# Counting edges by node and type elsewhere than in the sorts' permutations, in a four-layer graph kernel on one NeuronCore

## The chip, the cores and the metric

The kernel runs on 1 core of one Trainium2 chip. The metric is the device time of one execution in microseconds; of several runs the median is taken.

## The reference, cut to what matters

A graph of 3125 nodes and 50000 edges (src, dst, and a type of nine) passes four layers: ARMA convolution, GCN, a relational layer with two directions, and neighbour sums. Each sums rows of other nodes over the edges. The change touches what is prepared for them once: how many edges of each type leave and enter each node.

```python
seg = jnp.concatenate([edge_type * n + edge_index[0], (edge_type + R) * n + edge_index[1]])
count = jax.ops.segment_sum(ones, seg, num_segments=2 * R * n).reshape(2 * R, n, 1)
cnt = jnp.maximum(count, 1.0)
...
deg = jax.ops.segment_sum(jnp.ones(src.shape[0], jnp.float32), dst, num_segments=n)
dinv = jnp.where(deg > 0, jax.lax.rsqrt(jnp.maximum(deg, 1.0)), 0.0)
```

The relational layer divides by cnt and adds count times a bias; the first two layers scale by dinv, which comes from the counts by destination, summed over the types.

## The kernel before, in words

Nodes lie in 25 tiles of 128. All work runs in stages, one after the other, each with its own instruction stream for each engine and semaphores between them; there is no planner, the order is that of the code.

First the 50000 edges are sorted twice. `rank_stage` finds each edge's place (chunk and slot) in the list sorted by tile; `Permute` moves the edges there. The first sort (key 1) goes by destination, over 400 columns of 125 edges; the second (key 0) by source, over the 416 columns of the list that the first one left. `Permute.run_stage` takes U = 16 columns a turn, in two buffers: VectorE makes one-hots of 16 columns in one operation each (line 450: place, chunk, local, group) and weights the first WEIGHED = 8 columns' place one-hots with the edge's high value (line 459), ScalarE weights the other eight and all low values (lines 475, 477), and TensorE makes three matmuls for a column (lines 492, 496, 498): high and low, by chunk, 416 columns wide, and local by group, 225 wide. The last one counts edges by node (128 local places) and by tile and type (25 x 9 groups): in the first sort by destination, in the second by source. VectorE may begin a turn when TensorE has ended the turn two before (`moved`).

`end_stage` decodes the sorted list and copies the counts. `degree_stage` stands between the sorts and makes dinv from the counts by destination. The second `rank_stage` also turns x (7 groups of four tiles) and spreads dinv along a row (7 groups, 50 passes of line 367) on TensorE, evicted by ScalarE, before its ranking matmuls.

`staircase_stage` (lines 944 to 1161) lays out 576 items, each a chunk of the list with a block of 512 source nodes in a tile of destination nodes or the reverse; TensorE picks each item's values from the turned list (line 1035). It also lists the nodes with many edges (`heavy`, `clone`, lines 1104 to 1161). `pair_counts_stage` then adds up, for each of the 576 items, a one-hot of the source with a one-hot of the target, a matmul of 512 columns (line 1225) into a place of PSUM that is known only at run time. TensorE's sequencer loads such places from a table, 16 registers for DOZEN = 12 items (`load`, line 1187), and waits each FOUR = 4 items for VectorE (`made`, line 1222) and ScalarE (`freed`, line 1223). VectorE makes a target one-hot an item (line 1203) and source one-hots for 16 items at once (line 1199). ScalarE evicts finished blocks (line 1249) and clears PSUM (line 1237); SP and POOL store them to two tables.

`dense_stage` is the matmul of a table of pair counts with rows (line 1609); its first use, `sum_x`, also gathers the rows of the heavy nodes from both tables (POOL, lines 1480 and 1481), cuts their counts in two (line 1707) and writes the rest back. Each loop turn n takes one block of 128 rows, brought by SP in a ring of four (line 1531); VectorE runs steps of `beside` (the factors of the typed layer) in between.

## Time and profile before

| | |
|---|---|
| time, median of 3 runs | 4890.89 us (4884.92 to 4891.96) |
| span of the profiled execution, first to last instruction | 4357.4 us |
| the median less that span (the page has no time of the profiled execution beside its span) | 533.5 us |
| first sort's turns, 51 to 270 us | VectorE 209.69 busy, TensorE 196.12 |
| second sort's turns, 324.7 to 553 us | VectorE 219.28 busy, TensorE 202.35 |
| pair counts, 588 to 793 us | VectorE 194.96 busy, TensorE 144.86 |
| mean granted clock of TensorE | 0.783 |

Busy times are those of operations; loads of registers, address computations, waits and branches of a sequencer count as none, though they take time. They stand in the trace under their line with a q behind the engine (PEldq is TensorE's sequencer). PEclk is the granted clock as a share of 2.4 GHz. Times in the views are microseconds from the span's start, durations in a list of instructions nanoseconds.

### The profile page before, as it was taken

Reading aid. Unit: us, or ns where it says so; the run is one execution under the profiler, and the core shown is the slowest. Engines: PE = TensorE matmul, PEld = TensorE weight load, DVE = VectorE, ACT = ScalarE, POOL = GpSimd, SP = SyncE. Lnnn points to the kernel's source line nnn. Section 1 sums busy time; section 2 is a strip of 40 time slices with the busy share of each in tenths; the row PEclk is TensorE's granted clock in tenths of the full one; section 3 lists DMA queues with packets and bytes.
Section 4 is the critical chain, followed back from the end, with each engine's and each line's share of the span. In section 5 each row is a group of like instructions: output and inputs, shape, how many; then the busy total and the mean of one; then the engine's idle time right before and its main releaser. Section 6 shows DMA issues by size and latency. Waiting matters only on the chain. (4 is left out here: it accounts for less than half of the span.)

```text
span 4357.4 us, 56067 instructions
## 1 busy us (share of the span) xinstructions
PE 3257.6 (75%) x16061; PEld 2561.3 (59%) x16062; DVE 2284.6 (52%) x3880; ACT 1437.0 (33%) x2751; POOL 1758.1 (40%) x1969
## 2 busy tenths in 40 slices
PE   6978966689999879998993787866674644444459
PEld 3545522559999677796862676755552533333348
DVE  8989999514445643355683555543454622222224
ACT  5848848546666564564500000000000000000005
POOL 0000012101111011120166777777756777777751
PEclk8989989899999989999995656555577855555569
DMA  4000025828888475694673111122245111212226
GB/s 156 0 0 0 0 106 206 266 80 288 289 288 291 142 276 177 233 313 142 232 284 98 49 53 53 53 53 52 53 177 183 52 52 52 53 52 53 53 68 205
DMA packets 161460, 569.88 MB, mean 131 GB/s; under 512 B 46176, under 2 KB 54721, under 8 KB 160908
## 3 DMA queue, kind: packets, MB, share of 16 engines
q1 hardware_dynamic: 89494, 394.83, 26.2%
q0 software_dynamic: 71408, 172.45, 13.2%
q8 instruction: 77, 1.26, 0.1%
q14 instruction: 91, 0.75, 0.1%
q10 hardware_dynamic: 390, 0.60, 0.0%
HBM read 405.06 MB, written 162.66 MB: 130 GB/s over the span
## 5 line engine op out<-in xcount | busy, mean ns | idle before, releaser
L2027 PE MATMUL ps_sum_rgcn<-gathered_rgcn,select_sum_rgcn 128*128 x3328 | 972.3, 440 | 560.1 <-SPq L1918 492.0
L2027 PEld LDWEIGHTS ps_sum_rgcn<-gathered_rgcn,select_sum_rgcn 128*128 128x128 f32 x3328 | 762.0, 308 | 625.6 <-issue 624.5
L1609 PE MATMUL ps_sum_arma<-pair_counts_f_sum_arma,parts_sum_arma 128*128 128x448 f32 (+1 forms) x3850 | 856.7, 374 | 13.6 <-ACT pair_counts_f_sum_arma L1650 13.6
L1943 POOL DMA_INDIRECT gathered_rgcn<-by_dst,row x782 | 739.4, 946 | 238.4 <-issue 218.3
L1609 PEld LDWEIGHTS ps_sum_arma<-pair_counts_f_sum_arma,parts_sum_arma 128*128 128x128 f32 x3850 | 707.1, 189 | 72.2 <-issue 14.2
L1943 POOL DMA_INDIRECT gathered_rgcn<-by_src,row x558 | 527.6, 945 | 198.1 <-issue 154.2
L2066 ACT COPY acc_rgcn<-ps_sum_rgcn 128x128 f32<-128x128 f32 x100 | 26.6, 266 | 1639.4 <-PE ps_sum_rgcn L2027 1639.4
L1488 POOL DMA_DIRECT2D rows<-parts_sum_arma x275 | 153.2, 558 | 896.3 <-DVE parts_sum_arma L1697 855.7
L2103 DVE TENSOR_TENSOR select_sum_rgcn<-one_hot_sum_rgcn,ps_coef_sum_rgcn 128x2048 f32<-128x2048 bf16 x52 | 118.9, 2287 | 576.0 <-PE ps_sum_rgcn L2027 575.9
L477 ACT ACTIVATE low_one_hot_sort<-place_one_hot_sort,low_in_sort 128x128 f16<-128x128 f16 (+1 forms) x816 | 300.0, 425 | 124.4 <-DVE place_one_hot_sort L450 124.4
L492 PE MATMUL ps_sort<-chunk_one_hot_sort,high_one_hot_sort 128*128 128x416 f16 (+1 forms) x816 | 283.9, 348 | 46.7 <-DVE group_one_hot_sort L450 46.7
L1952 PE MATMUL ps_turn_sum_rgcn<-ident,one_hot_sum_rgcn 128*128 128x128 bf16 x832 | 245.2, 302 | 94.1 <-DVE one_hot_sum_rgcn L2075 41.8
L496 PE MATMUL ps_sort<-chunk_one_hot_sort,low_one_hot_sort 128*128 128x416 f16 (+1 forms) x816 | 282.5, 346 | 0.0
L2080 DVE COPY turned_sum_rgcn<-ps_turn_sum_rgcn 128x1024 bf16<-128x1024 bf16 x104 | 71.5, 688 | 386.3 <-PE ps_got_sum_rgcn L1959 353.8
L693 POOL DMA_INDIRECT gathered_rgcn<-by_src,row x224 | 216.5, 966 | 136.1 <-ACTq L759 71.2
L1650 ACT CAST pair_counts_f_sum_arma<-blocks_arma_mid 128x1792 fp32r<-128x1792 f16 x125 | 211.3, 1690 | 133.9 <-PE ps_sum_arma L1609 126.3
L2075 DVE TENSOR_TENSOR one_hot_sum_rgcn<-local,ps_iota_sum_rgcn 128x2048 bf16<-128x2048 f32 x104 | 237.4, 2284 | 7.4 <-DVE select_sum_rgcn L2103 1.8
L1000 POOL IOTA after_iota_staircase<- 128x128 f16 x1 | 0.2, 243 | 551.9 <-POOLq L509 551.9
L498 PE MATMUL ps_sort<-group_one_hot_sort,local_one_hot_sort 128*128 128x225 f16 (+1 forms) x816 | 215.3, 264 | 0.0
L1650 ACT CAST pair_counts_f_sum_arma<-axT_arma 128x1792 fp32r<-128x1792 f16 x100 | 169.1, 1691 | 124.6 <-PE ps_sum_arma L1609 119.5
L1959 PE MATMUL ps_got_sum_rgcn<-factor_parts,turned_sum_rgcn 128*128 x832 | 183.3, 223 | 20.8 <-DVE turned_sum_rgcn L2080 17.2
L1712 DVE CAST pair_counts_f_sum_arma<-blocks_arma_mid 128x1334 fp32r<-128x1334 f16 x125 | 106.9, 855 | 170.8 <-PE ps_sum_arma L1609 164.8
(458 smaller groups left out, 5283.9 us busy)
## 6 DMA issues: line engine op xcount, KB each, us to landing
blocks_arma_mid<-pairs SPq DMA_DIRECT2D x125, 800.0 KB, 5.9
axT_arma<-pairs SPq DMA_DIRECT2D x100, 800.0 KB, 5.9
pair_counts_arma_sum<-pairs SPq DMA_DIRECT2D x50, 800.0 KB, 6.0
rows<-parts_sum_arma POOLq DMA_DIRECT2D x275, 128.0 KB, 5.3
by_src<-rows_rgcn_tables SPq DMA_DIRECT2D x50, 576.0 KB, 3.8
by_dst<-rows_rgcn_tables SPq DMA_DIRECT2D x50, 576.0 KB, 3.8
exact<-whole_pairs SPq DMA_DIRECT2D x25, 800.0 KB, 3.3
pairs<-whole_pairs POOLq DMA_DIRECT2D x25, 800.0 KB, 5.5
```

Source lines behind the costliest of these rows:

```text
L477: nc.scalar.activation(self.low[e, parity, u // 2, :, u % 2], place, ACT.Copy, scale=o.low_in[e, bass.ds(i * U + u, 1)]).then_inc(self.wei ...
L492: nc.tensor.matmul(self.ps[:, 0, 0:C], self.high[e, parity, pair, :, at], chunk, start=False, stop=False)
L496: nc.tensor.matmul(self.ps[:, 1, 0:C], self.low[e, parity, pair, :, at], chunk, start=False, stop=False)
L498: nc.tensor.matmul(self.ps[:, 2, 0:self.G], self.local[e, parity, pair, :, at], self.group[e, parity, pair, :, at], start=False, stop=Fals ...
L693: nc.gpsimd.indirect_dma_start(got[:, n, :], None, tables[0].rearrange("n (r f) -> (n r) f", f=D), bass.IndirectOffsetOnAxis(ap=k.orders[0 ...
L1609: last = nc.tensor.matmul(ps[:, g, 0:here.stop - here.start], half(part), counts[:, n % 2, here].bitcast(F32R), start=t == 0 and part == 0 ...
L1650: nc.scalar.copy(counts[:, n % 2, 0:CUT].bitcast(F32R), ring[n % RING][:, 0:CUT]).then_inc(raised, 1)
L1943: nc.gpsimd.indirect_dma_start(got[:, n % PLACES, :], None, table, bass.IndirectOffsetOnAxis(ap=o.row[:, n % C:n % C + 1], axis=0)).then_i ...
L1952: inst = nc.tensor.transpose(ps_turn[:, half, v, :], hot[:, parity, half * OCTET + v, :], k.ident16[:, :])
L1959: inst = nc.tensor.matmul(ps_got[:, parity, at:at + PARTS * R], turned[:, half, v, :], parts[:, bass.ds(tile, 1), :, :].rearrange("p a q r ...
L2027: nc.tensor.matmul(ps[:, bass.ds(slot, P)], select[:, parity, u, :], rows[:, bass.ds(place, D)], start=False, stop=False, skip_group_check ...
L2075: nc.vector.tensor_tensor(hot[:, parity, :, :], k.local[:, bass.ds(first, U), None].to_broadcast([P, U, P]), ps_iota[:, None, 0:P].to_broa ...
```

## The change

The counts leave `Permute` in the form that they had, and come from two other places.

- **By destination (`k.count[:, :, R:]`), in the second sort.** Its columns come from the list sorted by destination, so that a column has one tile. The 225-wide group one-hot becomes one of 9 types (`type_in`), and the matmul of 9 columns goes to the tile's place in PSUM, `count_at`, of which 16 are loaded each turn. The first sort makes no counts at all: it has two matmuls a column. The weighting on VectorE grows to 14 columns of 16 in the first and 10 in the second sort.
- **By source (`k.count[:, :, 0:R]`), in the pair counts.** For each of the 576 items a second matmul, 9 columns wide, of the same source one-hot with a one-hot of the type (`typed`, made for 16 items at once), goes to a place from a second table `q.count_at`, 16 registers loaded for 12 items. The types of the items are a third pick in `staircase_stage`; edges outside the item's block get type 0 there, which no one-hot names.
- `degree_stage` goes; dinv is made at the end of the second sort. Its row is made in `staircase_stage`, no longer in `rank_stage`.
- The list of heavy nodes needs the counts by source and moves into `sum_x`, spread over its loop turns 4 to 11. The two gathers go from the start of POOL's queue to before its thirteenth store, the write back from SP's turn 9 to turn 21.

```diff
@@ rank_stage
-            nc.vector.tensor_copy(o.local_in[e, :], ints[e, 1, :])
-            nc.vector.scalar_tensor_tensor(o.group_in[e, :], tile_of[e, :], float(R), k.edges[e, 2, :], ALU.mult, ALU.add)
...
-            nc.vector.scalar_tensor_tensor(o.group_in[e, :], tile_of[e, :], float(R), l.type[e, :], ALU.mult, ALU.add)
+            nc.vector.tensor_copy(o.local_in[e, :], l.local[e, :])
+            nc.vector.tensor_copy(o.type_in[e, :], l.type[e, :])
+            nc.vector.tensor_scalar(o.count_at[:, :], l.tile_of_chunk[:, :], float(R), float(2 * SPAN), ALU.mult, ALU.add)
...
-                for g in range(2 * FOURS):
+                for g in range(FOURS):
                     tiles = four(g)
                     act.wait_ge(grouped, g + 1)
-                    to = k.xT if g < FOURS else k.dinv_row
-                    nc.scalar.copy(to[:, tiles.start * P:tiles.stop * P], ps[:, 3 + g % B, 0:len(tiles) * P]).then_inc(evicted, 1)
 @block.tensor
...
-                        place = ps[:, 3 + g % B, v * P:v * P + P]
-                        if g < FOURS:
-                            last = nc.tensor.transpose(place, k.xcur[:, t, :], k.ident[:, :])
-                        else:
-                            last = nc.tensor.matmul(place, k.ident[0:NT, t:t + 1].to_broadcast([NT, P]), dinvT[:, :],
-                                                    start=True, stop=True)
+                        last = nc.tensor.transpose(ps[:, 3 + g % B, v * P:v * P + P], k.xcur[:, t, :], k.ident[:, :])
                     last.then_inc(grouped, 1)
@@ Permute
+        self.weighed = 14 if o.key else 10
...
-                    compare(self.chunk, o.chunk_in, C)
-                    compare(self.local, o.local_in, P)
+                    if not o.key:
+                        compare(self.local, o.local_in, P)
+                        compare(self.type, o.type_in, R)
                     dve.wait_ge(self.placed, i + 1)
-                    nc.vector.tensor_tensor(self.high[e, parity, 0:self.WEIGHED // 2, :, :],
-                                            self.place[e, parity, 0:self.WEIGHED // 2, :, :],
-                                            columns(o.high_in, P, self.WEIGHED), ALU.mult)
-                    compare(self.group, o.group_in, self.G).then_inc(self.made, 1)
+                    nc.vector.tensor_tensor(self.high[e, parity, 0:self.weighed // 2, :, :],
+                                            self.place[e, parity, 0:self.weighed // 2, :, :],
+                                            columns(o.high_in, P, self.weighed), ALU.mult)
+                    compare(self.chunk, o.chunk_in, C).then_inc(self.made, 1)
...
+                    if not o.key:
+                        count_at = nc.values_load_multi_w_load_instructions(
+                            o.count_at[0:1, bass.ds(i * U, U)], engines=(PE,), min_val=2 * SPAN,
+                            max_val=2 * SPAN + (NT - 1) * R,
+                            skip_runtime_bounds_check_because="made from tiles below NT")[1]
                     pe.wait_ge(self.made, i + 1)
                     for u in range(U):
                         pair, at = divmod(u, 2)
                         chunk = self.chunk[e, parity, pair, :, at]
-                        if u >= self.WEIGHED:
+                        if u >= self.weighed:
                             pe.wait_ge(self.weighted, i * U + u + 1)
                         nc.tensor.matmul(self.ps[:, 0, 0:C], self.high[e, parity, pair, :, at], chunk, start=False,
                                          stop=False)
-                        if u < self.WEIGHED:
+                        if not o.key:
+                            nc.tensor.matmul(banks[:, bass.ds(count_at[u], R)], self.local[e, parity, pair, :, at],
+                                             self.type[e, parity, pair, :, at], start=False, stop=False,
+                                             skip_group_check=True)
+                        if u < self.weighed:
                             pe.wait_ge(self.weighted, i * U + u + 1)
                         nc.tensor.matmul(self.ps[:, 1, 0:C], self.low[e, parity, pair, :, at], chunk, start=False,
-                                         stop=False)
-                        nc.tensor.matmul(self.ps[:, 2, 0:self.G], self.local[e, parity, pair, :, at],
-                                         self.group[e, parity, pair, :, at], start=False, stop=False).then_inc(self.moved, 1)
-
+                                         stop=False).then_inc(self.moved, 1)
+
+                banks = self.ps[:, :, :].rearrange("p b w -> p (b w)")
                 nc.tensor.sem_inc(self.moved, 2 * U)
@@ end_stage
+                    then(nc.vector.tensor_copy(k.count[:, :, R:S2], ps[:, 2, 0:NT * R].rearrange("p (t r) -> p t r", r=R)))
+                    then(nc.vector.tensor_reduce(deg[:, :], k.count[:, :, R:S2], AX.X, ALU.add))
+                    nc.vector.tensor_scalar(has[:, :], deg[:, :], 0.0, None, ALU.is_gt)
+                    nc.vector.tensor_scalar_max(roots[:, 0, :], deg[:, :], 1.0)
+                    nc.vector.tensor_scalar(roots[:, 1, :], deg[:, :], 1.0, None, ALU.add).then_inc(rooting, 1)
...
-def degree_stage(nc, k):
...
@@ staircase_stage
+            pe.wait_ge(kept, 1)
             pe.wait_ge(moved, 1)
+            for g in range(FOURS):
+                if g >= 2:
+                    pe.wait_ge(evicted, g - 1)
+                for v, t in enumerate(four(g)):
+                    last = nc.tensor.matmul(ps[:, 6 + g % 2, v * P:v * P + P], k.ident[0:NT, t:t + 1].to_broadcast([NT, P]),
+                                            dinvT[:, :], start=True, stop=True)
+                last.then_inc(grouped, 1)
...
-            for n in (0, 1):
+            pe.wait_ge(evicted, FOURS)
+            for n in (0, 1, 2):
+                if n == 2:
+                    pe.wait_ge(shown, 1)
                 for first, w, bank in ((0, SPAN, 1), (SPAN, ITEMS - SPAN, 2)):
                     for h in range(QUARTERS):
-                        last = nc.tensor.matmul(ps[:, 5 * n + bank, 0:w], turned[:, n, h, :], pick[:, h, first:first + w],
+                        last = nc.tensor.matmul(ps[:, 5 * (n % 2) + bank, 0:w], turned[:, n, h, :], pick[:, h, first:first + w],
                                                 start=(h == 0), stop=(h == QUARTERS - 1))
-            last.then_inc(laid, 1)
-            pe.wait_ge(reached, 1)
-            nc.tensor.matmul(ps[0:1, 4, P:P + U], row[:, :], k.ident[0:U, 0:U], start=True, stop=True).then_inc(lined, 1)
-            pe.wait_ge(cloned, 1)
-            for t in range(NT):
-                last = nc.tensor.matmul(ps[:, 5, 2 * LOW:2 * LOW + 2], clone[:, t, :], place[:, t, :], start=(t == 0),
-                                        stop=(t == NT - 1))
-            last.then_inc(placed, 1)
...
+            last_target.then_inc(shown, 1)
+            dve.wait_ge(shown, 1)
+            then(nc.vector.tensor_scalar(inside[:, :], q.target_at[:, :], 0.0, None, ALU.is_ge))
+            then(nc.vector.scalar_tensor_tensor(inside[:, :], q.target_at[:, :], float(SPAN), inside[:, :], ALU.is_lt, ALU.mult))
+            dve.wait_ge(laid, 2)
+            for first, w, bank in ((0, SPAN, 1), (SPAN, ITEMS - SPAN, 2)):
+                here = slice(first, first + w)
+                nc.vector.tensor_tensor(q.type_at[:, here], inside[:, here], ps[:, bank, 0:w], ALU.mult)
@@ pair_counts_stage
+                    nc.vector.tensor_tensor(
+                        typed[:, n // V % 2, :, :, :],
+                        q.type_at[:, n:n + V].rearrange("p (a b) -> p a b", b=2)[:, :, None, :].to_broadcast([P, V // 2, R, 2]),
+                        q.steps[:, None, 1:R + 1, :].to_broadcast([P, V // 2, R, 2]), ALU.is_equal)
...
+                        counts = load(PE, count_at, i * (BODY // DOZEN * ROW) + u // DOZEN * ROW, ROW,
+                                      SPANS * SPAN + (NT - 1) * R)
                     if u % FOUR == 0:
 
                         pe.wait_ge(made, i * BODY + u + FOUR)
                         pe.wait_ge(freed, frees[u % DOZEN // FOUR])
                         nc.tensor.nop(nofuse=True)
+                    nc.tensor.matmul(ps[:, bass.ds(counts[u % DOZEN], R)], source[:, u // V % 2, u % V // 2, :, u % 2],
+                                     typed[:, u // V % 2, u % V // 2, :, u % 2], start=False, stop=False, skip_group_check=True)
                     nc.tensor.matmul(ps[:, bass.ds(table[u % DOZEN], SPAN)], source[:, u // V % 2, u % V // 2, :, u % 2],
                                      target[:, u % V, :], start=False, stop=False, skip_group_check=True).then_inc(multiplied, 1)
@@ dense_stage
-    CLONED = 9
+    HEAVY, LISTED, CLONED, CUTOUT, REPLACED = 4, 7, 12, 17, 21
...
-            if exact is not None:
-                at = bass.IndirectOffsetOnAxis(ap=k.clone_node[:, 0:1], axis=0)
-                nc.gpsimd.indirect_dma_start(clone_whole[:, :], None, exact[:, :], at).then_inc(k.cloned, 16)
-                nc.gpsimd.indirect_dma_start(clone_half[:, :], None, pairs[:, :], at).then_inc(k.cloned, 16)
             for b in range(M):
                 if b:
                     gp.wait_ge(fetched, 16 * (fetched_before + b))
                 for t in range(NT):
                     m = b * NT + t
+                    if exact is not None and m == CLONED:
+                        gp.wait_ge(listed, 1)
+                        at = bass.IndirectOffsetOnAxis(ap=k.clone_node[:, 0:1], axis=0)
+                        nc.gpsimd.indirect_dma_start(clone_whole[:, :], None, exact[:, :], at).then_inc(k.cloned, 16)
+                        nc.gpsimd.indirect_dma_start(clone_half[:, :], None, pairs[:, :], at).then_inc(k.cloned, 16)
                     gp.wait_ge(split, m + 1)
...
+                if exact is not None and n == HEAVY + 1:
+                    pe.wait_ge(ready, 1)
+                    nc.tensor.matmul(ps[:, 7, 0:NT], ones[:, :], heavy16[:, :], start=True, stop=True)
+                    nc.tensor.matmul(ps[:, 7, LOW:LOW + NT], before[:, :], heavy16[:, :], start=True, stop=True).then_inc(counted, 1)
+                if exact is not None and n == LISTED + 2:
+                    pe.wait_ge(cloned, 1)
+                    for i in range(NT):
+                        last = nc.tensor.matmul(ps[:, 7, 2 * LOW:2 * LOW + 2], clone[:, i, :], place[:, i, :], start=(i == 0),
+                                                stop=(i == NT - 1))
+                    last.then_inc(placed, 1)
...
+            def list_heavy():
+
+                dve.wait_ge(counted, 1)
+                then(nc.vector.tensor_copy(heavy_of[:, :], ps[:, 7, 0:NT]))
+                then(nc.vector.tensor_tensor_scan(upto[:, :], heavy_of[:, :], heavy_of[:, :], 0.0, ALU.add, ALU.max))
+                then(nc.vector.tensor_tensor(upto[:, :], upto[:, :], heavy_of[:, :], ALU.subtract))
+                then(nc.vector.tensor_tensor(upto[:, :], upto[:, :], ps[:, 7, LOW:LOW + NT], ALU.add))
+                then(nc.vector.scalar_tensor_tensor(where[:, :], upto[:, :], float(LAST + 1), heavy[:, :], ALU.add, ALU.mult))
+
+            def place_heavy():
+
+                then(nc.vector.tensor_tensor(clone[:, :, :], after_iota[:, None, :].to_broadcast([P, NT, P]),
+                                             where[:, :, None].to_broadcast([P, NT, P]), ALU.is_equal))
+                nc.vector.tensor_tensor(clone[0:LAST, NT - 1, :], clone[0:LAST, NT - 1, :], k.ident16[0:LAST, :],
+                                        ALU.add).then_inc(cloned, 1)
+
+            def name_heavy():
+
+                dve.wait_ge(placed, 1)
+                then(nc.vector.tensor_copy(found[:, :], ps[:, 7, 2 * LOW:2 * LOW + 2]))
+                nc.vector.scalar_tensor_tensor(k.clone_node[:, :], found[:, 1:2], float(P), found[:, 0:1], ALU.mult,
+                                               ALU.add).then_inc(listed, 1)
...
-                if n >= RING:
+                if exact is not None and n == HEAVY:
+                    find_heavy()
+                elif exact is not None and n == LISTED:
+                    list_heavy()
+                elif exact is not None and n == LISTED + 1:
+                    place_heavy()
+                elif exact is not None and n == LISTED + 4:
+                    name_heavy()
+                elif n >= RING:
                     next(apart, None)
                     next(apart, None)
```

## Rows read from the trace of the kernel before

**Rows 1.** Busy time by engine in stretches of the first 800 us, clock and DMA share behind
```profile
core 0: us, PE busy (x) PEld busy (x) DVE busy (x) ACT busy (x) POOL busy (x), PEclk, DMA share, GB/s
51.00:270.00 219.00, 196.12 (x1206) 116.17 (x1204) 209.69 (x129) 179.14 (x600) 0.00 (x0) 0.97 0.01 4
277.61:280.46 2.85, 0.00 (x1) 0.03 (x1) 1.44 (x9) 1.53 (x2) 0.00 (x0) 0.61 0.00 0
324.70:553.00 228.30, 202.35 (x1254) 121.48 (x1252) 219.28 (x137) 186.35 (x624) 0.00 (x0) 0.97 0.00 0
553.00:588.00 35.00, 13.34 (x77) 7.27 (x77) 32.15 (x89) 2.16 (x4) 2.98 (x4) 0.57 0.00 1
588.00:793.00 205.00, 144.86 (x583) 59.31 (x583) 194.96 (x614) 162.74 (x347) 46.55 (x24) 0.94 0.49 192
```

**Rows 2.** Timeline of VectorE, one turn of the first sort: start us, duration us
```profile
77.40 1.22 DVE L450 TENSOR_TENSOR place_one_hot_sort<-slot_in_sort,steps_sorts 125x2048 f16<-125x2048 f16 x1
78.53 3.62 DVE L450 TENSOR_TENSOR chunk_one_hot_sort<-chunk_in_sort,steps_sorts 125x6656 f16<-125x6656 f16 x1
82.07 1.22 DVE L450 TENSOR_TENSOR local_one_hot_sort<-local_in_sort,steps_sorts 125x2048 f16<-125x2048 f16 x1
83.20 0.68 DVE L459 TENSOR_TENSOR high_one_hot_sort<-place_one_hot_sort,high_in_sort 125x1024 f16<-125x1024 f16 x1
83.81 2.02 DVE L450 TENSOR_TENSOR group_one_hot_sort<-group_in_sort,steps_sorts 125x3600 f16<-125x3600 f16 x1
85.75 1.22 DVE L450 TENSOR_TENSOR place_one_hot_sort<-slot_in_sort,steps_sorts 125x2048 f16<-125x2048 f16 x1
```

**Rows 3.** Timeline of TensorE, one item of a turn
```profile
535.17 0.34 PE L492 MATMUL ps_sort<-chunk_one_hot_sort,high_one_hot_sort 128*128 128x416 f16 x1
...
535.53 0.26 PE L498 MATMUL ps_sort<-group_one_hot_sort,local_one_hot_sort 128*128 128x225 f16 x1
535.63 0.34 PE L492 MATMUL ps_sort<-chunk_one_hot_sort,high_one_hot_sort 128*128 128x416 f16 x1
```

**Rows 4.** Timeline of ScalarE, two activations of a turn
```profile
72.80 0.42 ACT L475 ACTIVATE high_one_hot_sort<-place_one_hot_sort,high_scale_sort 125x128 f16<-125x128 f16 x1
73.09 0.42 ACT L477 ACTIVATE low_one_hot_sort<-place_one_hot_sort,low_in_sort 125x128 f16<-125x128 f16 x1
```

**Rows 5.** Instructions of lines 1225, 1187, 588:793: ns min/median/max, first and last start
```profile
L1225 PEldq FUSED_REGOPS  x576: 37/37/37, 591.3 to 791.0; - x192
...
L1225 PE MATMUL ps_pairs<-target_one_hot_pairs,source_one_hot_pairs x576: 379/379/634, 592.1 to 792.9; 128*128 128x512 f16 x192
...
L1187 PEldq TENSOR_LOAD <-item_at_adjacency x48: 1102/1232/3373, 589.3 to 786.4; - x48
```

**Rows 6.** Instructions of line 1225, one dozen (640.7:642.75)
```profile
L1225 PEldq FUSED_REGOPS  x12: 37/37/37, 640.8 to 642.7; - x12
```

**Rows 7.** Timeline of TensorE in the pair counts, two dozens
```profile
633.63 2.76 PE L1225 MATMUL ps_pairs<-target_one_hot_pairs,source_one_hot_pairs 128*128 128x512 f16 x12 [0.83 <-DVE target_one_hot_pairs L1203]
637.22 2.76 PE L1225 MATMUL ps_pairs<-target_one_hot_pairs,source_one_hot_pairs 128*128 128x512 f16 x12 [0.83 <-DVE target_one_hot_pairs L1203]
```

**Rows 8.** Timeline of the staircase, VectorE's and TensorE's largest operations of the clone list
```profile
581.17 3.49 DVE L1140 TENSOR_TENSOR clone_staircase<-after_iota_staircase,clone_row_staircase 128x3200 bf16<-128x3200 f16 x1
...
584.97 0.79 PE L1042 MATMUL ps_staircase<-node_place_staircase,clone_staircase 128*128 128x2 bf16 x25 [2.71 <-DVE clone_staircase L1142]
```

**Rows 9.** Timeline of the second ranking, TensorE and VectorE
```profile
294.93 7.59 PE L367 MATMUL ps_rank<-dinv_turned_rank,ident 25*128 25x128 f32 x50
...
303.91 1.28 DVE L316 COPY best_rank<-ps_rank 128x416 f32<-128x416 f32 x2 [5.63 <-PE ps_rank L395]
```

**Rows 10.** Instructions of lines 1992 and 1967, neighbouring loads in the typed sum
```profile
L1992 PEldq TENSOR_LOAD <-ring_late x1: 1113/1113/1113, 2364.0 to 2364.0; - x1
...
L1967 PEldq TENSOR_LOAD <-look_at_late x1: 1110/1110/1110, 2365.3 to 2365.3; - x1
```

**Rows 11.** The first sum: timeline of ScalarE, and busy times of a later stretch
```profile
831.41 1.69 ACT L1650 CAST pair_counts_f_sum_x<-pair_counts_sum_x 128x1792 fp32r<-128x1792 f16 x1 [12.93 <-DMA pair_counts_sum_x<-pairs]
...
850.00:860.00 10.00, 10.00 (x51) 9.28 (x50) 7.21 (x26) 7.97 (x8) 2.89 (x4) 1.00 1.02 418
```

212 lines of the change are left out of this document (103 added, 109 removed).

## The prediction

> **What bounds the kernel now.** I read the table of stretches first [rows 1], because the change touches only the first 900 us. In both sorts VectorE is busy for 96% of the stretch and TensorE for 89 to 90%; in the pair counts VectorE is busy for 95% and TensorE for 71%. By this view VectorE binds everywhere, and work taken from it should pay one for one. Then I asked for single turns. One turn of a sort takes 8.35 us from one place_one_hot to the next (77.40 to 85.75), with no gap between VectorE's five operations [rows 2]. TensorE spends 0.46 us on an item in it: 0.18 for each of the two 416-column matmuls, 0.10 for the 225-column one [rows 3], 16 items in 7.4 us. ScalarE issues one activation each 0.29 us [rows 4], 24 of them in 7.0 us.
>
> The pair counts need a second view, that of the sequencer's own instructions, since busy shares leave them out. For twelve items TensorE's sequencer makes one load of 16 registers, at least 1.10 us long, three groups of waits, and one address computation (FUSED_REGOPS) for each matmul [rows 5, 6]. Two neighbouring dozens start 3.59 us apart (633.63 to 637.22), of which the matmuls themselves take 2.76 with the last one's drain: this gap is not TensorE's array and not VectorE, which is named as releaser but works ahead [rows 7]. Twelve addresses stand in 1.9 us [rows 6], and three groups of waits account for two breaks of about 0.3 in it: 0.115 to 0.12 for an address with its matmul's dispatch. With 1.27 for a load and the address ahead of it, 1.27 + 3 x 0.30 + 12 x 0.115 = 3.55, so the sequencer alone explains 3.59. Forty-eight dozens give 172 us of the 203.6 from the first load to the last matmul (589.3 to 792.9) [rows 5]; VectorE is busy for 195 [rows 1]. Both nearly bind. The remaining 31 are long loads (median 1.23, longest 3.37 [rows 5]), the fill, loop ends and waits.
>
> **The first sort.** VectorE loses local_one_hot (1.14 from start to start) and group_one_hot (1.95), and its weighting grows from 8 to 14 columns: 0.60 becomes 1.00, by the slope between the 1024- and 2048-element operations (0.68 and 1.22). It now must wait for place_one_hot's end before weighting, 0.12 more. From turn start to TensorE's start: 1.26 + 1.00 + 3.62 + 0.05 = 5.93. TensorE loses the third matmul, 0.37 an item; from its first matmul to VectorE's release two turns on: 15 x 0.37 + 0.34 + 0.14 = 6.03. Two buffers make these a loop, (5.93 + 6.03) / 2 = 5.98 a turn, just above TensorE's own 5.92. ScalarE has 18 activations, 5.3 us, below it. 24 x (8.35 - 5.98) + 2.5 at the first fill + 1.6 in the last turn: -61 us.
>
> **The second sort.** VectorE keeps local, gains a 144-element compare (0.15, an estimate from the slope; bounds 0.1 and 0.3), weights 10 columns (0.73) and loses group: 1.14 + 1.14 + 0.15 + 0.73 + 3.53 = 6.69, 6.82 to TensorE's start. The 9-column matmul is nearest to the 2-column ones of the clone list, 25 in 0.79 us with the drain, so 0.025 to 0.03 each [rows 8]; upper bound the 0.10 of today's. An item is 0.40, and 15 x 0.40 + 0.21 + 0.48 = 6.67. (6.82 + 6.67) / 2 = 6.75. ScalarE's 22 activations are 6.5 us, close below. Here too TensorE's sequencer gets a load and 16 addresses a turn, 1.3 + 1.9 us, but its other 48 dispatches are static and it waits for VectorE anyway: hidden, priced at nothing. Were the cover gone, it would add at most 1.3 a turn, 34 us. 25 x (8.35 - 6.75) + 1.6 + 0.9: -42.5.
>
> The rule of the Trainium skill that bears on the small matmuls is in "TensorE: Matmul & The Clock Gate", Back-to-back issue gap: up to 64 columns a matmul costs an issue floor of about 25 ns. The row of 25 matmuls agrees (0.025), but its addresses are constants. By that rule the 576 new matmuls of the pair counts would cost 14 us in all, and the result would be the first rival below.
>
> **Between the sorts.** The degree stage goes: -2.55 (277.61 to 280.16, most of the stretch in [rows 1]). Its seven small VectorE operations enter the end of the second sort, +1.0; the square root's table load lies behind ScalarE's copies there. In the rank stage 50 matmul passes of the dinv rows held TensorE for 7.59 us and VectorE idle for 5.63 [rows 9]; without them the ranking starts when its parts are ready: -5.3, -0.6 because three short 416-column operations on VectorE replace three longer ones, -0.3 from a shorter queue of transposes. -6.2 together.
>
> **The staircase.** The clone list leaves (VectorE's 3.49 us compare and what stands around it, 579.90 to 584.84 [rows 8]): -4.9. In its place TensorE makes the dinv rows before the picks: at the rate of [rows 9] 50 passes take 5.6 us at 2.4 GHz and twice that at 1.2, and this stretch runs at 0.57 [rows 1]. So the picks start some 3 to 8 us later, and a third pick, its waits, and five operations on VectorE follow (about 3 us). Net +2, bounds 0 and +6.
>
> **The pair counts.** VectorE: one 144-element compare each 16 items, 36 x 0.15 = 5 us; if VectorE still bound, that were all. TensorE's array: 576 x 0.03, not binding at either clock level. The sequencer: a second load of 16 registers each dozen and a second address each item. Two neighbouring loads of 16 in the typed sum start at 2364.0 and 2365.3 [rows 10]: they do not overlap, 1.3 each, 1.27 with the sum above. An address is 0.115. A dozen grows by 1.27 + 12 x 0.115 = 2.65, from 3.59 to 6.24, above VectorE's 4.1 (195 / 48); 48 x 2.65 = 127. The old remainder of 31 stays, but for the 2 to 4 us in which the sequencer waited for VectorE or ScalarE. I take +125; bounds +5 (all hidden) and +150 (each load as long as the median 1.23 or more, and transfers lengthening twice as many loads). Queued behind it are ScalarE's evictions and the stores of the rows; they have slack, as their pace is set by the same matmuls.
>
> **The first sum.** The two gathers of clone rows leave its start, where ScalarE waits 12.9 us for the fifth block of pair counts behind the transfer of dinv_loop in pieces of one number each [rows 11]. That transfer stays; without 1.6 MB ahead of it (two gathers of 128 rows of 6400 bytes), it starts and ends about 4 us earlier, at the 418 GB/s of a later stretch. Moved to the thirteenth row store on POOL, the gathers wait for the list; row stores queue behind them, with eight buffers in hand. VectorE's 6.7 us of list work fall in a stretch in which TensorE is busy for 10.00 us of 10.00 and VectorE for 7.21 [rows 11]; the 25 small matmuls add 0.7. Net -3, bounds -6 and +4.
>
> **Sum.** -61 - 42.5 - 2.6 - 6.2 + 1.0 + 2 + 125 - 3 = +12.7. The profiled span is 4357.4; what lies around it, 533.5 by the median 4890.9, I leave unchanged: 4903.6.
>
> **Rivals.** (1) Other side, faster: the sequencer works ahead of the array, as it does in the sorts, and the new loads and addresses hide there; the pair counts grow by VectorE's 5 us only. Result 4890.9 - 112 + 5, about 4784 (by the page's floor 4793). Against it: 3.59 us is the sequencer's own sum. It decides below 112 us of growth, 2.34 us a dozen. Chance 0.08. (2) One of the two prices is not paid (the second load overlaps the first, 61 us, or an address shares its computation with its neighbour's, 66): about 4840. Chance 0.10. (3) The sorts gain less: three engines within 0.3 us of each other wait for one another in turn, 6.4 and 7.1 us a turn; +19, 4923. For it: the loop through both buffers already costs more than each engine. Chance 0.12. (4) Transfers lengthen the doubled loads by as much again as today (some 23 us): 4927. Chance 0.10. The forecast has 0.60, with its own range of 4890 to 4918.
>
> **Chances and range.** A measurement here tells a change of over 0.2% (9.8 us) from none. Of the forecast's 0.60, 0.35 lie above 4900.7, 0.23 within the bound, 0.02 below. Rivals 1 and 2 are faster, 3 and 4 slower but for 0.02. Faster 0.20, same 0.25, slower 0.55. Leaving out rivals 1 and 2, the range reaches from 4878 to 4928.
>
> **What would show it.** In the profile after: 5.9 to 6.1 us from one place_one_hot to the next in the first sort, 6.6 to 6.9 in the second; 6.2 to 6.4 us between dozens of pair matmuls, two TENSOR_LOADs a dozen, 1152 address computations with 0.115 between them, and VectorE idle there for a third of the time; some 325 us from first load to last matmul. The prediction is wrong if dozens stand under 5.9 us apart (faster), or if the pair stage keeps VectorE's pace.

## The result and the profile after

The changed kernel takes 4922.97 us (median of four, 4913.22 to 4924.57), the kernel before, measured along with it, 4891.43 (four runs, 4884.92 to 4896.42). The ratio is 1.0066 with a 95% interval of 1.005 to 1.0081: slower by 31.5 us (24 to 40 by the interval). The forecast was +12.7 us, with a range from 4878 to 4928.

First the busy times by engine of the changed kernel, in the stretches that answer to [rows 1]: the first sort's turns, what lies between the sorts, the second sort's turns with its end, the staircase, and the pair counts from the first register load to the last matmul. The columns are those of [rows 1]: busy time of TensorE, of its weight loads, of VectorE, ScalarE and POOL, then clock, DMA share and GB/s.

```profile
50.67:213.00 162.33, 152.06 (x804) 77.85 (x802) 147.30 (x82) 135.32 (x450) 0.00 (x0) 0.97 0.01 6
213.00:257.00 44.00, 29.80 (x129) 14.76 (x130) 38.73 (x111) 4.56 (x9) 0.00 (x0) 0.77 0.00 1
257.00:444.00 187.00, 172.61 (x1264) 94.48 (x1263) 178.27 (x143) 172.03 (x574) 0.00 (x0) 0.97 0.00 0
444.00:485.80 41.80, 24.54 (x106) 17.63 (x105) 30.23 (x84) 7.07 (x14) 2.83 (x3) 0.56 0.00 1
485.80:828.30 342.50, 217.43 (x1160) 106.92 (x1158) 215.69 (x648) 167.85 (x347) 15.37 (x24) 0.80 0.30 115
```

Two places changed much, in opposite directions. The second sort begins at 257.0 us where it began at 324.7, and the pair counts' first load stands at 485.8 where it stood at 589.3 [rows 5]: 103.5 us are won by then. The pair counts then take 342.1 us to their last matmul (485.8 to 827.9), not 203.6: 138.5 us are lost. No engine is busy in them for more than 217 us of 342. In [rows 1] VectorE was busy for 95% of this stretch; now it is for 63%, and TensorE, with twice the matmuls, for 63% too. What fills the rest stands in no column of this view.

It stands in the rows of the sequencer. These are the loads and address computations of the whole stage (count; shortest, median and longest in ns; first and last start in us), to be read beside [rows 5].

```profile
L1164 PEldq TENSOR_LOAD <-item_at_adjacency x48: 1102/1107/3538, 485.8 to 820.2; - x48
L1164 PEldq ALU_OP  x48: 36/36/36, 486.9 to 821.9; - x48
L1164 PEldq TENSOR_LOAD <-count_at_adjacency x48: 1100/1105/3292, 487.0 to 821.9; - x48
...
L1210 PEldq FUSED_REGOPS  x576: 37/37/37, 488.5 to 826.6; - x192
...
L1212 PEldq FUSED_REGOPS  x576: 37/37/37, 488.6 to 826.7; - x192
```

There are 96 loads and 1152 addresses, twice what there was. The same view for one dozen, between 577 and 586 us:

```profile
L1164 PEldq TENSOR_LOAD <-item_at_adjacency x2: 1107/2080/3052, 577.9 to 584.2; - x2
...
L1164 PEldq TENSOR_LOAD <-count_at_adjacency x1: 1105/1105/1105, 579.2 to 579.2; - x1
```

A dozen whose two loads are both short takes 6.3 us (577.9 to 584.2), and its second load begins 1.3 us after the first, when that has ended. Over all 48 dozens the closest two stand 6.21 us apart (3.57 before). The forecast for this spacing was 6.24. The median, which has long loads and waits in it, grew from 4.12 to 6.62. Some loads are long, though, up to 3.5 us: the 96 sum to 144.2 us, which is 38.2 above 96 x 1.105; the 48 of before summed to 76.6, 23.6 above 48 x 1.105.

The sorts, in VectorE's timeline (start us, duration us; idle time before it and what ended it in brackets). The first sort, two turns and the start of a third, beside [rows 2]:

```profile
149.84 1.22 DVE L435 TENSOR_TENSOR place_one_hot_sort<-slot_in_sort,steps_sorts 125x2048 f16<-125x2048 f16 x1 [0.37 <-PE ps_sort L491]
151.19 1.09 DVE L445 TENSOR_TENSOR high_one_hot_sort<-place_one_hot_sort,high_in_sort 125x1792 f16<-125x1792 f16 x1
152.20 3.62 DVE L435 TENSOR_TENSOR chunk_one_hot_sort<-chunk_in_sort,steps_sorts 125x6656 f16<-125x6656 f16 x1
155.73 1.23 DVE L435 TENSOR_TENSOR place_one_hot_sort<-slot_in_sort,steps_sorts 125x2048 f16<-125x2048 f16 x1
157.08 1.09 DVE L445 TENSOR_TENSOR high_one_hot_sort<-place_one_hot_sort,high_in_sort 125x1792 f16<-125x1792 f16 x1
158.09 3.62 DVE L435 TENSOR_TENSOR chunk_one_hot_sort<-chunk_in_sort,steps_sorts 125x6656 f16<-125x6656 f16 x1
162.07 1.23 DVE L435 TENSOR_TENSOR place_one_hot_sort<-slot_in_sort,steps_sorts 125x2048 f16<-125x2048 f16 x1 [0.36 <-PE ps_sort L491]
```

Lengths of 5.89 (149.84 to 155.73) and 6.34 us (155.73 to 162.07) alternate, 6.11 on average. One is VectorE's own length; in every other it waits 0.36 us for TensorE to release the buffer. The second sort, one turn:

```profile
352.86 1.23 DVE L435 TENSOR_TENSOR place_one_hot_sort<-slot_in_sort,steps_sorts 128x2048 f16<-128x2048 f16 x1
354.00 1.22 DVE L435 TENSOR_TENSOR local_one_hot_sort<-local_in_sort,steps_sorts 128x2048 f16<-128x2048 f16 x1
355.14 0.22 DVE L435 TENSOR_TENSOR type_one_hot_sort<-type_in_sort,steps_sorts 128x144 f16<-128x144 f16 x1
355.28 0.82 DVE L445 TENSOR_TENSOR high_one_hot_sort<-place_one_hot_sort,high_in_sort 128x1280 f16<-128x1280 f16 x1
356.02 3.62 DVE L435 TENSOR_TENSOR chunk_one_hot_sort<-chunk_in_sort,steps_sorts 128x6656 f16<-128x6656 f16 x1
359.55 1.22 DVE L435 TENSOR_TENSOR place_one_hot_sort<-slot_in_sort,steps_sorts 128x2048 f16<-128x2048 f16 x1
```

It takes 6.69 us; with its neighbour of 6.74 the mean is 6.72. The compare of types takes 0.14 from start to start.

Last, TensorE in the staircase, beside [rows 8, 9].

```profile
463.12 11.03 PE L1002 MATMUL ps_staircase<-dinv_turned_staircase,ident 25*128 25x128 f32 x50
...
474.66 4.00 PE L1014 MATMUL ps_staircase<-pick_staircase,turned_staircase 104*128 104x512 f16 x16 [0.20 <-ACT wide_row L1033]
...
480.17 2.10 PE L1014 MATMUL ps_staircase<-pick_staircase,turned_staircase 104*128 104x512 f16 x8 [1.38 <-DVE target_at_adjacency L1117]
```

The 50 matmul passes of dinv's rows, 7.59 us in the second ranking, take 11.03 here, where the mean granted clock is 0.56 of 2.4 GHz, near the lower level of 1.2. The passes start 0.213 us apart here; in the second ranking of before some 30 of the 50 stood 0.112 apart, the others 0.213. The picks wait behind them, and the third pick comes only after a wait of 1.38 us for VectorE.

### The profile page after: what moved, and what is told of

Same layout as the page of the kernel before. It is cut to its first block and busy times, and to the rows that moved or that the text cites. A ratio compares the mean times of both kernels' runs of the same rounds, so it can differ in the third digit from the quotient of the medians.

```text
span 4911.9 us, 57120 instructions
## 1 busy us (share of the span) xinstructions
PE 3303.8 (67%) x16248; PEld 2538.4 (52%) x16249; DVE 2205.5 (45%) x3872; ACT 1384.1 (28%) x2550; POOL 1725.5 (35%) x1968
## 5 line engine op out<-in xcount | busy, mean ns | idle before, releaser
L2082 PE MATMUL ps_sum_rgcn<-gathered_rgcn,select_sum_rgcn 128*128 x3328 | 962.3, 422 | 649.3 <-issue 596.6
L2082 PEld LDWEIGHTS ps_sum_rgcn<-gathered_rgcn,select_sum_rgcn 128*128 128x128 f32 x3328 | 739.5, 291 | 729.6 <-issue 726.3
L2014 PEld LDWEIGHTS ps_got_sum_rgcn<-factor_parts,turned_sum_rgcn 128*128 128x128 bf16 x832 | 113.7, 137 | 372.1 <-issue 332.3
L463 ACT ACTIVATE low_one_hot_sort<-place_one_hot_sort,low_in_sort 128x128 f16<-128x128 f16 (+1 forms) x816 | 273.3, 425 | 87.7 <-DVE place_one_hot_sort L435 86.1
L716 DVE TENSOR_TENSOR rows_rgcn_tables<-ps_rgcn_tables,typed_bias_late 128x384 f32<-128x384 f32 x300 | 162.8, 556 | 182.8 <-remote 94.4
L1184 DVE TENSOR_SCALAR target_one_hot_pairs<-wide_adjacency,target_at_adjacency 128x512 f16<-128x512 f16 x576 | 170.0, 347 | 83.3 <-PE ps_pairs L1212 70.5
```

The costliest lines, as they stand in the source:

```text
L463: nc.scalar.activation(self.low[e, parity, u // 2, :, u % 2], place, ACT.Copy, scale=o.low_in[e, bass.ds(i * U + u, 1)]).then_inc(self.wei ...
L1184: nc.vector.tensor_scalar(target[:, n % V, :], q.wide[:, :], q.target_at[:, n:n + 1], None, ALU.is_equal).then_inc(made, 1)
L2014: inst = nc.tensor.matmul(ps_got[:, parity, at:at + PARTS * R], turned[:, half, v, :], parts[:, bass.ds(tile, 1), :, :].rearrange("p a q r ...
L2082: nc.tensor.matmul(ps[:, bass.ds(slot, P)], select[:, parity, u, :], rows[:, bass.ds(place, D)], start=False, stop=False, skip_group_check ...
```

## The experiments

All of them are made from the changed kernel, but for the first, which is the kernel before once more.

**A second trace of the kernel before.** The first trace's span, 4357.4 us, did not fit the runs' 4891.

> The kernel before, unchanged, for a second trace. The profiled span of before was 4357.4 us against a median of 4891, and that of the changed kernel 4911.9 against 4923. If the first trace was the odd one, this one shows a typed sum about 2337 us long (first to last instruction), as the changed kernel has, and not 1868; up to the typed sum its stages should stand within 1 us of the first trace. If the changed kernel's typed sum is slower because of the change, it shows 1868 again.

It took 4901.44 us with a span of 4900.1. The typed sum in the first trace of before, in this one, and in the changed kernel, in the view of stretches:

```profile
2352.00:4222.00 1870.00, 1128.99 (x5371) 943.97 (x5371) 736.44 (x690) 57.12 (x207) 1375.21 (x1452) 0.58 0.24 68
```

```profile
2406.00:4765.00 2359.00, 1153.16 (x5371) 933.29 (x5371) 739.24 (x690) 56.79 (x207) 1373.31 (x1452) 0.59 0.19 54
```

```profile
2434.00:4773.00 2339.00, 1139.58 (x5373) 922.15 (x5374) 739.42 (x690) 56.62 (x207) 1373.62 (x1452) 0.60 0.20 55
```

The last two last some 2335 to 2355 us, with nearly the same busy times as the first, which had 1866. Up to the pair counts' last matmul the two traces of before differ by 0.3 us (792.9 and 792.6), at the end of the first sum by 2.9. So the first trace is sound for the stages that the argument rests on. The second half of the expectation did not hold all the way: the stage ahead of the typed sum, which makes its tables, took 215 us (2194.1 to 2409.3) and not 165 (2190.8 to 2355.4). The 533.5 us that the prediction laid around the span lay inside it in a usual execution: some 490 us are time that the typed sum lacked in that first one, some 50 time that its tables lacked. Why, these runs do not show. The later stages also differ by some 20 us between two usual traces, so that only the first 930 us are compared trace with trace here, and the total by the medians.

**No counts by source.** The second load, the count matmul and the one-hot of types are left out; the counts by source stay zero.

```diff
-                        counts = load(PE, count_at, ...)
...
-                    nc.tensor.matmul(ps[:, bass.ds(counts[u % DOZEN], R)], source[...], typed[...], ...)
```

> The changed kernel without the counts by source (no second load, no count matmul, no one-hot of types; these counts stay zero). Theory of the sequencer's sum: dozens 3.6 us apart, 204 us from the first load to the last matmul, as before the change, and a total of about 4923 - 138 = 4785 us. Rival, that something else in the changed kernel (the third pick, the clock after a shorter second sort) slows the pair counts: over 215 us.

4780.09 us, ratio to before 0.9779 (0.9758 to 0.98). The stage takes 202.0 us from first load to last matmul (487.4 to 689.4), its closest dozens stand 3.57 us apart. So the loss lies wholly in what the change adds here, and all the rest of the change is worth 110 us. The rival, something else in the changed kernel, is refuted.

**A constant place, no load.**

```diff
-                        counts = load(PE, count_at, ...)
...
-                    nc.tensor.matmul(ps[:, bass.ds(counts[u % DOZEN], R)], source[...], typed[...], ...)
+                    nc.tensor.matmul(ps[:, SPANS * SPAN:SPANS * SPAN + R], source[...], typed[...], ...)
```

> The changed kernel with the count matmul at one constant place and without its load (all counts by source fall into the first tile's place). Theory: loads and address computations are the cost, not the matmuls; a constant matmul costs the sequencer 0 to 0.06 us, so dozens stand 3.6 to 4.3 us apart and the stage takes 204 to 220 us, near VectorE's own 200. Rival, any second matmul costs the 0.115 us: 5.0 us a dozen, about 267 us.

```profile
485.60:697.60 212.00, 165.21 (x1160) 77.68 (x1158) 198.89 (x648) 162.82 (x347) 44.66 (x24) 0.93 0.48 186
```

212.0 us with all 1160 matmuls, each with its own load of weights (1158 in the second column). Five hundred and seventy-six matmuls of 9 columns, their weight loads and 36 compares cost 10 us against none. Neither the array nor the weights are what costs 138. VectorE is busy for 94%, almost without a pause, as before the change.

**A place from a register, no load.** The two runs differ in whether the count matmul's place can share the address of the pair matmul.

```diff
-                    nc.tensor.matmul(ps[:, bass.ds(counts[u % DOZEN], R)], source[...], typed[...], ...)
+                    nc.tensor.matmul(ps[:, bass.ds(table[u % DOZEN], R)], source[...], typed[...], ...)
```

> The changed kernel without the second load; the count matmul takes its place from the item's own register (it adds into the pair counts, which are then wrong, and counts by source stay zero). Theory: 24 addresses a dozen, 3.59 + 12 x 0.115 = 4.97 us apart, stage about 48 x 4.97 + 28 = 267 us. Rival, an address is shared with its neighbour or hidden: 3.6 to 4.2 us and 204 to 215 us.

The stage took 207.8 us (486.2 to 694.0), as the rival has it. But the rows show that the run did not do what it was made for: the only address computations stand under the count matmul's line, and the pair matmul has none.

```profile
L1208 PEldq FUSED_REGOPS  x576: 37/37/37, 488.4 to 692.0; - x192
```

Two matmuls from one register use one computation. Hence the second form:

```diff
+        beside = ps[:, 16:(SPANS + 1) * SPAN]
...
+                    nc.tensor.matmul(beside[:, bass.ds(table[u % DOZEN], R)], source[...], typed[...], ...)
```

> The changed kernel without the second load; the count matmul takes the item's own register, but 16 columns further on, so that its place has to be computed by itself (the pair counts are wrong by it, counts by source stay zero). In the run with the shared register the trace had one address computation an item. Theory of the sequencer's sum: with two an item, 12 x 0.115 more, 4.97 us a dozen, about 48 x 4.97 + 28 = 267 us. Rival, the second computation hides: 208 to 215 us, as with the shared one.

```profile
L1210 PEldq FUSED_REGOPS  x576: 46/46/51, 487.5 to 766.6; - x192
...
L1212 PEldq FUSED_REGOPS  x576: 37/42/42, 487.6 to 766.7; - x192
```

281.6 us (485.3 to 766.9), 73.8 more than with the shared address, and again with 48 loads only. Its closest dozens stand 5.12 us apart, not 4.97. The address computations of an item last 46 and 42 ns here where the changed kernel's last 37 and 37, and follow each other after 0.120 and 0.124 us, not 0.115. That is 0.17 us a dozen, close to the 0.15 more; why they are longer was not tested. The second address of an item is paid in full.

**The second load.** The first attempt kept the load and gave the matmul a constant place.

```diff
-                    nc.tensor.matmul(ps[:, bass.ds(counts[u % DOZEN], R)], source[...], typed[...], ...)
+                    nc.tensor.matmul(ps[:, SPANS * SPAN:SPANS * SPAN + R], source[...], typed[...], ...)
```

> The changed kernel with its second load, but the count matmul at one constant place (all counts by source fall into the first tile's place). The two runs before showed 212 us for the stage with neither, 208 with the item's address shared. Theory: a second load adds 1.20 us to a dozen of 3.6 to 3.7, so 4.9 us at least, and about 48 x 4.9 + some 40 us of long loads = 275 us; VectorE, at 4.1 a dozen, no longer binds. Rival, a load by itself hides behind the array's work and only the pair of load and address is dear: under 225 us.

215.3 us, and only this load in its trace, 48 times:

```profile
L1164 PEldq TENSOR_LOAD <-item_at_adjacency x48: 1102/1196/3332, 486.3 to 695.0; - x48
```

The load whose registers nobody reads is not in the trace. The run therefore says nothing of the load; it is the run without load once more, and shows how far two traces of that may differ (212.0 and 215.3). So one address of each dozen was taken from the table:

```diff
+                    at = bass.ds(counts[0], R) if u % DOZEN == 0 else slice(SPANS * SPAN, SPANS * SPAN + R)
+                    nc.tensor.matmul(ps[:, at], source[...], typed[...], ...)
```

> The second load for real: in the run with the constant place its registers were used nowhere and the trace shows 48 loads, not 96. Here the first count matmul of each dozen takes its place from the loaded table and the other eleven a constant one (most counts by source fall into the first tile's place). Theory of the sequencer's sum: 1.27 for the load and 0.115 for one address on top of 3.6 to 3.7 us, 5.0 a dozen; stage 48 x 5.0 + some 35 us of long loads = 275 us. That is 63 above the 212 with neither; the changed kernel's 342 less the 281.6 with an address of its own gives 60.5 for the same load. Rival, the load hides when its registers are hardly used: under 230.

```profile
L1164 PEldq TENSOR_LOAD <-count_at_adjacency x48: 1100/1105/3516, 486.6 to 767.3; - x48
```

288.3 us, 13 more than expected and 76.3 more than the 212.0 without load and address. The closest dozens stand 5.00 us apart, as expected. What was too low is the time of long loads: the 96 loads sum to 147.6 us, 41.6 above 96 x 1.105, where the run without the second load had 26.0 above its 48 x 1.105.

**Stores out of the way.** The 50 transfers of finished rows (two of 0.8 MB for each of 25 tiles) wait until the last row is taken, and ScalarE no longer waits for a stored buffer before it fills it again. They then send the buffers of the last two rows; the tables in memory lack the others.

```diff
-                        act.wait_ge(kept[i % 2], (i // 2) * 16)
-                        act.wait_ge(stored[i % 2], (i // 2) * 16)
+                        pass
...
-                gp.wait_ge(taken, (i + 1) * SPANS)
+                gp.wait_ge(taken, NT * SPANS)
...
-                sp.wait_ge(taken, (i + 1) * SPANS)
+                sp.wait_ge(taken, NT * SPANS)
```

> The changed kernel with all 50 row stores of the pair counts issued after the last row is taken (they then store the last two rows' buffers, so the pair counts in memory are wrong). Theory: the store transfers are what lengthens register loads; without them all 96 loads take 1.10 to 1.11 us, the 38 us above that go, and the stage from first load to last matmul takes about 304 us; the stores follow after it, so the total is longer or equal. Rival, loads are long for another reason (the loop's turn, instruction fetch): 342 again.

```profile
L1164 PEldq TENSOR_LOAD <-item_at_adjacency x48: 1102/1105/1108, 487.8 to 784.5; - x48
...
L1164 PEldq TENSOR_LOAD <-count_at_adjacency x48: 1100/1105/1105, 489.1 to 785.8; - x48
```

and, in the view of stretches, from the first load to the last matmul:

```profile
487.80:791.60 303.80, 207.88 (x1159) 108.43 (x1158) 213.27 (x648) 167.82 (x347) 0.00 (x0) 0.85 0.00 0
```

Not one load is longer than 1.11 us, and the stage takes 303.8 us, 38.3 less than with the stores. This is the clearest row of the study: 48 x 6.25 = 300 us by the sequencer's sum (6.25 is the median here, 6.22 the closest), at VectorE 70% and TensorE 68% busy. The whole kernel takes 4951.59 us, since the stores now stand in front of the first sum.

**Narrower loads.**

```diff
-                        counts = load(PE, count_at, i * (BODY // DOZEN * ROW) + u // DOZEN * ROW, ROW, ...)
+                        counts = load(PE, count_at, i * (BODY // DOZEN * ROW) + u // DOZEN * ROW, DOZEN, ...)
```

> The changed kernel, its second load taking the 12 registers that are used and not 16. By the slope between loads of 16 registers (1.10 us) and of 8 to 9 (0.55) in the trace of before, 0.069 us a register: 0.28 us less a dozen, 5.98 apart, stage about 13 us shorter, 329. Rival, a load has one price whatever its width: 342 again.

```profile
L1164 PEldq TENSOR_LOAD <-count_at_adjacency x48: 845/848/2659, 488.2 to 810.1; - x48
```

329.0 us (486.9 to 815.9), 13.1 less, where two traces of the same pair counts differ by 2 (342.1 and, in the run on the second sort below, 344.1). Four registers fewer save 0.257 us, 0.064 each. The total of this one run, 4911.48 us, is 11.5 below the changed kernel's median, within the spread of single runs.

**The second sort's load and addresses.** The prediction priced them at nothing.

```diff
-                        count_at = nc.values_load_multi_w_load_instructions(o.count_at[0:1, bass.ds(i * U, U)], ...)
...
-                            nc.tensor.matmul(banks[:, bass.ds(count_at[u], R)], self.local[...], self.type[...], ...)
+                            nc.tensor.matmul(banks[:, 2 * SPAN:2 * SPAN + R], self.local[...], self.type[...], ...)
```

> The changed kernel with the count matmul of the second sort at one constant place, without its load of 16 registers (counts by destination wrong). The prediction priced load and addresses there at nothing, as VectorE and the array bind at 6.7 us a turn. Theory: the turn stays at 6.71 us within 0.05. Rival, part of the sequencer's 3.1 us a turn shows: 6.4 or less, 8 us or more over 26 turns.

```profile
352.76 1.23 DVE L435 TENSOR_TENSOR place_one_hot_sort<-slot_in_sort,steps_sorts 128x2048 f16<-128x2048 f16 x1
...
359.46 1.23 DVE L435 TENSOR_TENSOR place_one_hot_sort<-slot_in_sort,steps_sorts 128x2048 f16<-128x2048 f16 x1
```

Turns of 6.70 and 6.74 us, mean 6.72, with and without; from the first turn's start to the last's it is 169.8 us here and 169.7 in the changed kernel. There the trace has 26 loads and 416 addresses, and they cost nothing that these runs can tell:

```profile
L473 PEldq TENSOR_LOAD <-count_at_sort x26: 1102/1106/1294, 257.1 to 430.9; - x26
...
L486 PEldq FUSED_REGOPS  x416: 37/37/37, 263.8 to 437.3; - x139
```

**Keep the half that pays.** Counts by destination come from the second sort, as in the changed kernel; counts by source from the first, 225 columns wide, as the kernel before made those by destination there. The pair counts and the staircase make none, and the third pick is gone.

```diff
+            nc.vector.tensor_copy(o.local_in[e, :], ints[e, 2, :])
+            nc.vector.scalar_tensor_tensor(o.group_in[e, :], ints[e, 3, :], float(R), k.edges[e, 2, :], ALU.mult, ALU.add)
...
+                        if o.key:
+                            low = nc.tensor.matmul(self.ps[:, 2, 0:NT * R], self.local[...], self.type[...], ...)
```

> A version that keeps the half that pays: counts by destination in the second sort as in the changed kernel; counts by source in the first sort, 225 columns wide, as the kernel before counts there by destination; none in the pair counts, and no third pick. Against the changed kernel: first sort's turns back to 8.35 us (+54), pair counts back to 203 us (-138), third pick gone (-3): 4923 - 87 = 4836 us, 0.989 of before. Rival, that the sorts' gain is one of both sorts together or that the longer first sort costs more than in the kernel before (its source codes are made in the first ranking): 4860 or more.

Its stretches: first sort's turns and end, second sort's, pair counts.

```profile
50.60:265.00 214.40, 191.85 (x1180) 113.94 (x1179) 208.93 (x125) 179.13 (x600) 0.00 (x0) 0.97 0.01 4
314.60:502.00 187.40, 173.32 (x1261) 95.20 (x1260) 178.27 (x142) 171.60 (x573) 0.00 (x0) 0.96 0.00 0
540.90:749.30 208.40, 149.71 (x583) 60.63 (x582) 194.59 (x612) 162.77 (x347) 40.24 (x24) 0.92 0.48 189
```

4841.01 us where 4836 was expected, 0.9902 of the kernel before (0.9883 to 0.9922), 82 us below the changed kernel. Turns are 8.35 us in the first sort and 6.72 in the second, the pair counts take 208.4.

## Why the prediction came out as it did

The direction, the mechanism and the outer range (4878 to 4928) held; the size did not. The measured +31.5 us is two and a half times the forecast +12.7, and 4922.97 lies above the forecast's own range of 4890 to 4918, where the prediction had put rivals 3 (4923) and 4 (4927). That it falls on rival 3's figure is chance, as the terms show. In the traces the loss at the last matmul of the pair counts is 35.0 us (827.9 against 792.9). Term by term:

- **Sorts, degree stage and ranking**: forecast -61 - 2.6 - 6.2 = -69.8 up to the second sort's start, measured -67.7 (257.0 against 324.7). The turn is 6.11 us and not 5.98. The loop through both buffers that the prediction computed is there, as the alternating 5.89 and 6.34 show, but it is longer than reckoned: 6.03 us from a turn's start to TensorE's first matmul (forecast 5.93) and 6.20 from there to the release (forecast 6.03), together 0.27 for two turns; 24 turns make 3 us of it.
- **Second sort, its end and the staircase**: forecast -42.5 + 1.0 + 2 = -39.5, measured -35.8 (228.8 us from the sort's start to the first load, 264.6 before). The turn is right, 6.72 against 6.75 (15 x 0.40 + 0.21 + 0.48 is 6.69 and not 6.67, which moves the 6.75 by 0.01 at most), and so is the load priced at nothing, as its own run shows. The staircase is what was too cheap: the dinv rows stand ahead of the picks for 11.03 us, the upper of the two rates that the prediction named, and VectorE waits 3.9 us at their end where the old kernel had work on the clone list. From the second sort's last matmul to the first load it is 46.1 us, 39.0 before: 7.1 more where +3 was forecast (+1.0 at the sort's end, +2 here). With the +1.0 as forecast the staircase costs about +6, the upper bound, in place of +2.
- **Pair counts**: forecast +125, measured +138.5. The repeated part is right almost to the digit: the closest dozens grow from 3.57 to 6.21 us, by 2.64 where 2.65 was forecast, 127 us in all. The runs that add one price at a time show that both are paid. For an address of its own it is 73.8 us (66 forecast; its addresses were the longer ones). For the load it is 60.5 by 342.1 - 281.6, where the changed kernel has the shorter addresses, and some 70 by 288.3 - 212.0 with 5.5 off for one address a dozen, the stretching included in both; 61 was forecast without it. The step that failed in its size is the one that read "The old remainder of 31 stays, but for the 2 to 4 us in which the sequencer waited". The remainder is made of two things that behave differently. What the loads take above 1.105 us grew from 23.6 to 38.2 us: the 48 loads that were there before have 25.4 of it, the 48 new ones 12.7, under the same row stores; what is waited for VectorE and ScalarE, with fill and loop ends, shrank from 8.6 to 5.8 (203.6 - 48 x 3.57 - 23.6, and 342.1 - 48 x 6.21 - 38.2). That is +14.6 - 2.8, where the prediction had -2. Rival 4 is this mechanism, at 14.6 us in place of its 23. That the stores are what stretches the loads is shown for the changed kernel: without them the excess is zero.
- **First sum**: forecast -3. Its last matmul stands 102.3 us after that of the pair counts; in the two traces of before it was 101.9 and 105.1. The term can't be told from zero, nor from its forecast.

The misses of the first three all point one way, 2.1 + 3.7 + 13.5 = 19.3 us. At the last matmul of the first sum the changed kernel stands 35.4 us behind the first trace of before and 32.5 behind the second (930.2 against 894.8 and 897.7), 23 and 20 more than forecast; the medians of the runs say 19.

What the stores cost the kernel before is not shown. Between its first and last one-hot in the pair counts VectorE was busy for 193 of 197 us:

```profile
590.30:787.30 197.00, 139.77 (x569) 57.38 (x567) 192.85 (x610) 158.63 (x340) 46.55 (x24) 0.95 0.50 195
```

VectorE's work and the sequencer's sum with its long loads came out alike there, and neither alone would have made the stage much shorter. The change took that cover away: in the changed kernel a stretched load counts in full (38.3 us saved for 38.2 of excess).

**The rivals.** The first, that sequencer work hides, is refuted in the pair counts and true in the second sort. The instructions are the same; what stands beside them differs: in the sort the turn is 6.7 us of VectorE against some 3 us of the new sequencer work, in the pair counts the sequencer's own sum bound already, level with VectorE. The prediction's decision point, 2.34 us of growth a dozen, was passed at 2.64. The second, one price unpaid, is refuted: neither the loads overlap (1.3 us apart) nor does an address share its computation, unless it is the same register and offset. The third happened in small: the first sort's turn is 0.13 us longer than forecast where it had 0.4, the second's is not; 3 of its 19 us.

The rule of the Trainium skill that the prediction weighed ("TensorE: Matmul & The Clock Gate", Back-to-back issue gap) is not contradicted by what the runs show. With constant places two in three of the 9-column matmuls start 25 to 27 ns before their neighbour, and 576 of them cost 10 us with their compares, below the 14 that its floor gives in a row, as the array does not bind there. The cost here lies ahead of the array, in making the address.

## What to carry to other kernels

Before moving an operation to a place where an engine looks idle, write down the sequencer's own sum there: register loads, one address computation for each place that is known at run time only, waits. A matmul whose place comes from a register can cost four times its array time (0.115 to 0.13 us against 0.025 to 0.03 between the starts of a 9-column matmul and its neighbour), and the busy columns show nothing of it; where another engine binds with room to spare, as in the second sort, it was free. Split what is left over in a stage by its causes, and ask of each whether it grows with the instruction that is doubled and whether it was covered before; long loads grow, and come out from under their cover.

## What was not expected of the hardware

- A load of 16 registers is stretched from 1.1 to as much as 3.5 us while row stores are under way, and returns to 1.10 to 1.11 without exception when they are not. In the changed kernel this is 38 us. Not every transfer does it: in the typed sum of before, at 68 GB/s, 312 such loads took 1.12 us at most.
- With TensorE waiting for its loads, less clock is granted: 0.80 of 2.4 GHz in the pair counts, 0.94 before. It costs little here: the closest dozens stand 6.21 us apart at 0.80 and 6.22 in the run without stores, which had 0.85 and fitted the sequencer's sum to within 4 us.
- A load costs by the register: 1.105 us for 16 and 0.848 for 12 on TensorE, 0.547 for 8 on ScalarE, 0.064 to 0.075 us for each register between them.
- In the run with a shifted base the shifted address takes 46 ns and the other one of the item 42, where both take 37 in the changed kernel.
